# Last 64 columns of two experts' output joins made together on the two column halves of TensorE, in the second attention of a transformer tower

## What is computed

```python
E, NH, WIN = (4, 12, 64)              # 4 attention experts of 12 heads of 16
for e in range(wq.shape[0]):
    q, k, v = x @ wq[e].T, x @ wk[e].T, x @ wv[e].T     # split into heads
    scores = jnp.where(mask, einsum('bhqd,bhkd->bhqk', q, k) * scale, NEG)
    o = einsum('bhqk,bhkd->bhqd', softmax(scores), v)
    outs.append(o @ wo[e].T)                            # the join, 192 columns
fused = jnp.concatenate(outs, axis=-1)                  # 768 columns
return silu(fused @ w_gate.T) * (fused @ w_up.T)
```

## Time and profile before

| | us |
|---|---|
| runs shown | 402.86, 403.28, 409.09 |
| median | 403.28 |
| profiled execution, its own time | 402.34 |
| its span (first to last instruction) | 400.6 |
| TensorE busy in the span | 381.1 (95%) |
| VectorE busy | 242.4 (61%) |
| ScalarE busy | 174.0 (43%) |
| the second attention's loop and what is behind it, about | 107.5 to 207.7 |

### The profile page before, as it was taken

The page is one execution under the profiler, slowest core; times in us unless marked ns, Lnnn a source line. Parts: engine busy times, 40 slices in busy tenths (PEclk is TensorE's granted clock), DMA queues, the critical chain, the costliest instruction groups (busy, mean ns, idle before and its releaser), DMA issues.

```text
span 400.6 us, 8785 instructions
## 1 busy us (share of the span) xinstructions
PE 381.1 (95%) x3602; PEld 312.7 (78%) x3602; DVE 242.4 (61%) x712; ACT 174.0 (43%) x304; POOL 69.2 (17%) x113
## 2 busy tenths in 40 slices
PE   8999999999899899979999899999999999999993
PEld 8988779779567566656557798899899898888783
DVE  1567756803499887896344568557558207676344
ACT  1256552561466666744435716225324310541420
POOL 7140010430023221331101400000000200304003
PEclk9999999999999999999999999999999999989997
DMA  8999800000259500000006984404401000000001
GB/s 205 263 202 218 176 15 2 1 2 0 53 171 269 136 2 2 2 4 2 2 0 176 269 227 139 130 11 137 139 7 53 2 0 2 2 2 2 0 2 39
DMA packets 28725, 30.69 MB, mean 77 GB/s; under 512 B 4867, under 2 KB 24137, under 8 KB 28686
## 3 DMA queue, kind: packets, MB, share of 16 engines
q1 hardware_dynamic: 28220, 29.96, 29.8%
q10 hardware_dynamic: 306, 0.17, 0.2%
q0 software_dynamic: 160, 0.01, 0.0%
HBM read 29.73 MB, written 0.39 MB: 75 GB/s over the span
## 4 chain that ended last, share of the span: by engine, by line
PE 77%; DVE 12%; ACT 4%; issue 4%; POOL 2%; DVEq 0%; POOLq 0%
PE ps L1529 68%; PE ps L1533 6%; PE ps L1541 4%; DVE front L1199 2%; DVE front L1189 2%; DVE front L1188 1%; DVE bn L1029 1%; POOL rstd L525 1%; DVE front L1177 1%; DVE wide L1394 0%; DVE xn L1044 0%; ACT front L687 0%; ACT front L805 0%; DVE front L1179 0%; DVE mv L1032 0%
## 5 line engine op out<-in xcount | busy, mean ns | idle before, releaser
L1529 PE MATMUL ps<-halves 128*128 128x512 f32 (+2 forms) x380 | 84.1, 376 | 1.3 <-ACT front L743 1.3
L1529 PEld LDWEIGHTS ps<-halves 128*128 128x128 f32 x380 | 66.6, 188 | 13.4 <-ACT front L743 1.7
L1529 PE MATMUL ps<-wide,front 128*128 128x192 f32 x432 | 72.0, 327 | 0.0
L1529 PEld LDWEIGHTS ps<-wide,front 128*128 128x128 f32 x432 | 70.3, 190 | 1.0 <-issue 0.5
L1529 PEld LDWEIGHTS ps<-front 64*32 64x32 f32 (+3 forms) x1488 | 51.4, 132 | 20.0 <-issue 11.6
L1529 PE MATMUL ps<-front 64*32 64x64 f32 (+3 forms) x1488 | 60.0, 241 | 5.8 <-issue 2.1
L743 ACT ACTIVATE front<-ps,colc 128x512 f32<-128x512 f32 x60 | 39.7, 688 | 53.8 <-PE ps L1529 53.7
L569 POOL TENSOR_TENSOR front<-front 128x768 f32<-128x768 f32 x16 | 23.6, 1472 | 75.8 <-DVE front L1200 75.8
L1332 DVE SCALAR_TENSOR_TENSOR xn<-ps,small,xn 128x192 f32<-128x192 f32 x28 | 9.8, 411 | 28.0 <-PE ps L1529 28.0
L1189 DVE TENSOR_TENSOR front<-front 128x768 f32<-128x768 f32 x16 | 23.9, 1493 | 0.5
L1529 PE MATMUL ps<-xT,turned 128*64 128x256 f32 (+1 forms) x96 | 22.6, 458 | 0.8 <-ACT front L781 0.8
(11 more groups left out here) (280 smaller groups left out, 553.3 us busy)
## 6 DMA issues: line engine op xcount, KB each, us to landing
wide<-in_w SPq DMA_DIRECT2D x8, 576.0 KB, 4.5
wide<-in_w SPq DMA_DIRECT2D x8, 384.0 KB, 5.7
wide<-in_w SPq DMA_DIRECT2D x16, 192.0 KB, 6.3
front<-in_a2w SPq DMA_DIRECT2D x5, 576.0 KB
front<-in_a1w SPq DMA_DIRECT2D x5, 384.0 KB
front<-in_x SPq DMA_DIRECT2D x3, 512.0 KB, 7.4
front<-in_w_qkv SPq DMA_DIRECT2D x2, 576.0 KB, 7.1
front<-in_a1w SPq DMA_DIRECT2D x5, 192.0 KB
```

The source lines that it names most:

```text
L1529: return pe.matmul(o, l, r, start=start, stop=stop)
```

## The change

The ends of the joins are no longer made expert by expert. `join(e)` makes the top alone, and the new `join_ends(g)` makes the ends of experts 2g and 2g + 1, in turn on partitions 0 to 63 and 64 to 127 of one bank. For this the heads of two experts have to be kept: `headsT` puts expert 2's heads into two slices of `fT` that nothing else uses. ScalarE copies the ends of experts 0 and 1 with one instruction of 128 partitions (`fT_ends`) where there were two of 64 partitions and a third for expert 2; VectorE's copy of the last end has 128 partitions where it had 64. The semaphore counts follow (`TOP_OF`).

The other work of the steps moves:

| step | before | after |
|---|---|---|
| (1,1) | join 0, top and end | join 0, top |
| (2,1) | join 1, top and end | join 1, top |
| (2,2) | first half of values of expert 3 | ends of experts 0 and 1 |
| (2,3) | second half of values of expert 3 | both halves of values of expert 3 |
| (3,0) | join 2, top and end | gate_up of tile 2, three chunks |
| (3,1) | gate_up of tile 2, four chunks | join 2, top |
| (3,2) | gate_up of tile 3, four chunks | gate_up of tile 2, one chunk, and of tile 3, four |
| behind the loop | join 3, top and end | join 3, top; ends of experts 2 and 3 |

```diff
+            def join(e):
+                pe.wait_ge(s["oT1_done"], NT * (e + 1))
+                join_free(e)
                 for h in range(2):
-                    ins = mm(ps[at:at + n, bank, :], woT[e][0:96, h, r0:r0 + n], oT1[0:96, e % 2, h, :], h == 0, h == 1)
+                    ins = mm(ps[:, 6 if e == EA - 1 else 2, :], woT[e][0:96, h, 0:P], headsT[e][0:96, h, :], h == 0, h == 1)
+                ins.then_inc(s["wo1_mm"], 1)
+
+            def join_ends(g):
+                join_free(2 * g + 1)
+                for h in range(2):
+                    for e in (2 * g, 2 * g + 1):
+                        at = DB * (e % 2)
+                        ins = mm(ps[at:at + DB, (5, 0)[g], :], woT[e][0:96, h, P:D], headsT[e][0:96, h, :], h == 0, h == 1)
                 ins.then_inc(s["wo1_mm"], 1)
...
-            first = ((0, 0), (1, 0), (2, 0), (0, 1))
+            first = ((0, 0), (1, 0), (0, 1), (2, 0))
...
+                elif t == 0:
+                    pe.wait_ge(s["fT_top"], 2)
+                    pe.wait_ge(s["v1_done"], 2 * EA)
+                    gate_up(2, first[:3])
+                elif t == 1:
+                    join(e - 1)
...
             gate_up(1, first)
-            join(EA - 1, 0)
-            join(EA - 1, 1)
+            join(EA - 1)
+            join_ends(1)
```

More of the change, by code:

```diff
@@ L66, in v_bank @@
     return lane(e) if j else 5
+TOP_OF = (1, 2, 4, 5)
 TURN_OF = {1: 1, 2: 2, 3: 4, 4: 5, 5: 6}
@@ L168, in vit_tower @@
         fT = take(EA, 2, T)
+        headsT = oT1[:, 0], oT1[:, 1], fT[:, 1:4:2, 1, :], oT1[:, 0]
         last_at = 19600
@@ L796, in oT_out @@
                 act.wait_ge(s["pv1_mm"], n + 1)
-                if e >= 2 and t == 0:
-                    act.wait_ge(s["wo1_mm"], 2 * (e - 1))
-                act.activation(oT1[0:96, e % 2, :, t * P:(t + 1) * P].rearrange("p c (m i) -> p c m i", m=2),
+                if e == EA - 1 and t == 0:
+                    act.wait_ge(s["wo1_mm"], 3)
+                act.activation(headsT[e][0:96, :, t * P:(t + 1) * P].rearrange("p c (m i) -> p c m i", m=2),
                                ps[0:96, 6:8, 0:P].rearrange("p m (c i) -> p c m i", c=2),
@@ L843, in _ @@
                 e, t = divmod(n, NT)
-                both = e == 0 and t == 1 or e == 1 and t == 2
+                both = e < EA - 1 and t == e + 1
                 pT1_out(n)
@@ L853, in _ @@
                     qk_out(3, 0)
-                elif e == EA - 2 and t >= 2:
-                    v_out(e + 1, t - 2)
-                if e >= 1 and t == (1 if e < EA - 1 else 0):
+                if e >= 1 and t == 1:
                     fT_out(e - 1)
+                elif e == 2 and t == 2:
+                    fT_ends()
                 if n + 2 < N1:
@@ L1209, in w1_low, with fT_low @@
                                   ALU.subtract).then_inc(s["w1_lo"], 1)
[L1211 to L1215, removed]
+            def fT_low():
+                dve.wait_ge(s["wo1_mm"], 6)
+                dve.tensor_copy(fT[:, 2, 1, :], ps[:, 0, :]).then_inc(s["fT_end"], 1)
             dve.wait_ge(s["qk1_mm"], 3)
@@ L1233, in _ @@
             w1_low(1)
-            fT_low(EA - 1)
+            fT_low()
             def gated(g):
@@ L1920, in values_in @@
                 pe.wait_ge(s["qk1_done"], 3 * e + 2 + j)
-                if e >= 2:
-                    pe.wait_ge(s[("fT_end", "fT_top")[j]], e - 1)
+                if j == 1 and e >= 2:
+                    pe.wait_ge(s["fT_top"], e - 1)
+                if j == 0 and e == EA - 1:
+                    pe.wait_ge(s["fT_end"], 1)
                 for m in range(2):
@@ L1968, in values1, with join_free @@
                 ins.then_inc(s["pv1_mm"], 1)
[L1970 to L1982, removed]
-                for h in range(2):
-                    ins = mm(ps[at:at + n, bank, :], woT[e][0:96, h, r0:r0 + n], oT1[0:96, e % 2, h, :], h == 0, h == 1)
+            def join_free(e):
+                if e + 2 < EA:
+                    pe.wait_ge(s["qk1_done"], 3 * (e + 2) + 3)
+                elif e < EA - 1:
+                    pe.wait_ge(s["v1_done"], 2 * EA)
+            def join(e):
+                pe.wait_ge(s["oT1_done"], NT * (e + 1))
+                join_free(e)
+                for h in range(2):
+                    ins = mm(ps[:, 6 if e == EA - 1 else 2, :], woT[e][0:96, h, 0:P], headsT[e][0:96, h, :], h == 0, h == 1)
[6 more added lines that the diff above has]
+                        ins = mm(ps[at:at + DB, (5, 0)[g], :], woT[e][0:96, h, P:D], headsT[e][0:96, h, :], h == 0, h == 1)
                 ins.then_inc(s["wo1_mm"], 1)
@@ L2011, in _ @@
                     project1(e + 1, 2)
-                elif e == 0 and t == 1 or e == 1 and t == 2:
+                elif e < EA - 1 and t == e + 1:
                     values_in(e + 1, 0)
@@ L2016, in _ @@
                     project1(2, t - 2)
-                elif t == (1 if e < EA - 1 else 0):
-                    join(e - 1, 0)
-                    join(e - 1, 1)
+                elif e < EA - 1 and t == 1:
+                    join(e - 1)
                 elif e == 1:
@@ L2022, in _ @@
                     project1(3, 1)
-                elif e == EA - 2:
-                    values_in(e + 1, t - 2)
-                elif t < 3:
+                elif e == 2:
+                    join_ends(0)
+                elif t == 0:
+                    pe.wait_ge(s["fT_top"], 2)
+                    pe.wait_ge(s["v1_done"], 2 * EA)
+                    gate_up(2, first[:3])
+                elif t == 1:
+                    join(e - 1)
+                elif t == 2:
                     pe.wait_ge(s["fT_top"], EA - 1)
-                    pe.wait_ge(s["fT_end"], EA - 1)
-                    gate_up(t + 1, first)
+                    gate_up(2, first[3:])
+                    gate_up(3, first)
                 else:
```

11 lines of the change are left out of this document (5 added, 6 removed).

## The result

The changed kernel takes 399.38 us in the median of six runs (397.24 to 399.99), the kernel before 403.25 (402.86 to 409.09). The ratio is 0.9897 with a 95% interval of 0.9868 to 0.9926, so between 3.0 and 5.3 us less. Forecast were 399.3 us and 4.0 us less.

A forecast was written before the change was run, and what follows sets the result against it. TensorE was taken to bind heavy steps, VectorE light ones. Four ends at 1.86 go, two pairs at 1.9 come, 3.6 us less work; the walk gave 4.0, so 403.28 - 4.0 = 399.3 us, range 397.6 to 401.8.

The forecast's parts named there:

- The likeliest case: Forecast as walked through the pipeline steps: 4.0 us less, 398.6 to 400.2 us, chance 0.58.
- The price of a pair: TensorE's ends of two experts, eight records on two column halves, take 1.9 us; bounds 1.8 and 3.7.
- Not overlapping: Rival: the column halves don't run at once, a pair takes 3.7 us, time 402.1 us; chance 0.05.
- slower: Rival: weight loads and matmuls wait for each other, 4.8 us a pair, time 404.3 us; chance 0.02.
- The walk: New starts computed through steps 5 to 15 of the four-engine pipeline; last transposes at 188.0 against 191.98, 4.0 us less.
- in(7): Start of VectorE's read of scores `softmax1_in(7)`, forecast unchanged at 140.96; other numbers name the later reads.
- The exchanged wait: Step 12: gate_up waits 0.85 us for ScalarE's values copy, replacing expert 2's join waiting 1.08 for the heads.
- TensorE last at step 15: TensorE reaches step 15's transposes at 188.0, after GpSimd's side at 187.7; before the change they started at 191.98.
- The remainder moves as a block, and later transfers are released by steps that move with it: Everything behind step 15's last transposes shifts unchanged, so the 4.0 us gained reach the end.
- The clock: Rival: the lower-clock stretch at 354 to 358 falls away or elsewhere; 1.2 us, 398.1 if away; chance 0.12.
- the stall of TensorE with "issue" as its reason: TensorE's one bare stall, 1.39 us at 135.71, which may fall on other instructions.

The follow-up runs named there:

- steady kernels: Kernel before and changed kernel, both with expert 3's first weights loaded earlier and the sixteen small records split into two groups: 401.38 and 397.87 us.
- e1_after_again: The changed kernel run again without an edit: 398.16 us, ratio 0.9896 to the kernel before.
- e3: Changed kernel with both matmuls of one expert's end ahead of both of the other, not in turn: 399.88 us, ratio 0.9942; stage 63.28 us.
- e7: Changed kernel with GpSimd's cut of the decay table moved behind the loop: 399.10 us; stage 63.04 us, 0.23 less.
- e4: Changed kernel with ScalarE's second copy of expert 3's values ahead of the exponential in step (2,3): 397.81 us, ratio 0.9883; stage 62.53 us.
- e2: Kernel before with the paired ends alone, joins, values and gate_up left in their old steps: 400.51 us, ratio 0.9935; stage 63.68 us.
- early load: Changed kernel with the load of expert 3's first weights issued as soon as its slot is free: 399.53 us over twelve runs, ratio 0.9929.
- e11_all_steady: Changed kernel with values copies ahead of the exponential, decay-table cut behind the loop, expert 3's first weights loaded early, small records split: 396.60 us, ratio 0.9840.

## Why the prediction was right, point by point

- **The likeliest case came, with the size off by a seventh.** Walked were 4.0 us in the stage, measured 3.42 (first traces) and 3.51 (medians of the steady kernels). The median of 399.38 against the forecast of 399.3 is in part luck: the medians of the first comparison differ by 3.87 us, of which the stage gave 3.42, and in `e1_after_again` they differ by 4.67 with the same stage.
- **The price of a pair.** Forecast were 1.9 us, bounds 1.8 and 3.7; the row says 1.94. It was right to take the form in the earlier trace rows for the measure and not the Trainium skill's rule on row groups (TensorE: Matmul & The Clock Gate, Part 3), with which the trace doesn't agree. Not overlapping (402.1) and slower (404.3) are excluded by this row, and by the second pair's 1.87. I had put weight on the order of the halves as in `project1`; e3 shows that it plays no part.
- **The walk, step by step**, each as a distance from in(7), forecast and measured: in(8) 4.50 and 4.49; in(9) 9.00 and 8.99; in(10) 15.5 and 15.66; in(12) 24.5 and 24.64; in(13) 29.0 and 29.35; in(14) 33.5 and 33.84; in(15) 38.4 and 39.07; transposes of step 14 42.2 and 42.89; of step 15 47.0 and 47.59. Where VectorE sets the pace, up to in(9), the walk hits to 0.01. In steps 10 and 11 it writes 169.2 and 174.3 for the end of the scores, where its own prices add up to 169.0 and 174.2; VectorE sets the next read in both, so nothing hangs on it.
- **Where the 0.55 us went.** 0.21 us is the one step of VectorE that took 4.71: I had noted no place where GpSimd's work slows VectorE's, and e7 gives it back. About 0.3 is in step 12: from in(14) to gate_up 1.48 us and not 1.35, three chunks in 2.10 and not 2.0, and 0.11 from the end of the scores to VectorE's read (180.25 to 180.36), which the walk left out. The same 0.11 makes up the 0.1 at in(10). Some 0.1 came back in step 14. In the kernel before, in(13) came 4.56 us after in(12), so the cut cost next to nothing: VectorE was itself 1.07 us late there, and the cut ended at 169.28, a microsecond before the scaling began at 170.27.
- **The exchanged wait.** "This 0.85 takes the place of the 1.08": 0.84 in the trace. It was worth looking for what stands ahead of the copy on ScalarE; e4 shows it cost 0.74 us.
- **TensorE last at step 15**: right, no wait before 188.88, and behind it the block was moved without change: 15.68 us to the filler against 15.67.
- **The moves of the steps** I had not priced apart. They are worth 0.4 us (e2).
- **"The remainder moves as a block, and later transfers are released by steps that move with it"**: the step of the prediction that was wrong in the first trace. The filler came 3.09 us sooner, the transfer's issue 2.51 and ScalarE's work on it 1.11, and ScalarE's order passed that on to TensorE: 0.76 us. In the six other traces of changed stages without the early load there is no such stall.
- **The clock**: I named the place near 355, where it fell in all but four of the thirteen traces. I had not named the place behind the sixteen small records, where a fall cost 1.7 us in four traces and 3.35 in one. Nor is the clock the only source of the spread: ahead of in(7) the thirteen traces differ by 2.3 us, of which up to 0.8 is the stall of TensorE with "issue" as its reason that the prediction names (1.39 us before, 0.56 to 1.18 in the changed stages).

## What to carry to other kernels

If two products have 64 output rows each, try them together on the two column halves of TensorE: the eight records here took about as long as four (rows of 1.94 and 1.88 us). Then follow the wait that is moved, not only the one removed: a copy that stands behind an exponential in its queue cost 0.74 us where the whole gain was 3.42, and exchanging two instructions gave it back. Where runs scatter more than the effect, measure the stage between two marks in the trace, list the mean clock of every run beside its time, and don't take three good traces for a steady kernel.

## What the runs showed of the hardware

- Matmuls on different column halves overlap even when two of one half stand ahead of two of the other in the queue (e3: eight records in 1.94 us in both orders). Their weight loads, on the same rows, lie beneath: eight loads of 0.13 to 0.14 us each in that time.
- A float32 VectorE subtraction of 768 elements with two inputs took 0.96 us where GpSimd did nothing (111.20 in the changed kernel), 1.52 where GpSimd's multiplication ran beside it for 0.70 us, 1.58 to 1.59 at 0.77 and 1.74 at 0.92. In each of these it ends 0.81 to 0.82 us after the multiplication does. By these numbers it gets 0.15 us of its own 0.96 done while both run, however long that is, and the rest behind it: it stands still for most of the overlap and isn't slowed in proportion. VectorE's 4.50 us a step have 0.56 of this in them. Why the two engines meet, these runs don't show.

```profile
111.20 0.96 DVE L1194 TENSOR_TENSOR front<-front 128x768 f32<-128x768 f32 x1
```

- Some 2.8 us of matmuls on 8 and 3 rows, in the middle of dense work, were followed in five of ten traces by a granted clock at the lower of its two levels for 3.4 us or more, at a price of 1.7 us or more; split in two groups, in none of three traces. That the split is the reason isn't shown: three of six runs of `e11_all_steady`, which has it, were 2.1 to 3.5 us longer than the shortest at mean clocks of 0.984 to 0.986 in place of 0.997 to 0.998.
